# Turning the quantised feed-forward weights inside the attention stage, and moving the moments out of the feed-forward's turns

## The chip, the cores and the metric

The kernel runs on one core of a Trainium2 chip. The metric is the device time of one execution in microseconds (us); smaller is better.

## What is computed

Eight sequences of 384 tokens with 256 channels pass through two layers. Cut to what matters here:

```
h = concat(edge rows of the image, text)              # 8 x 384 x 256
h = h + attention0(layernorm(h))                      # 16 heads, two kinds of keys
h = h + feedforward0(layernorm(h))                    # blockwise FP4 of inputs, weights and hidden
h = h + attention1(layernorm(h))                      # 64 anchors for each of 16 heads
h = h + experts(layernorm(h))                         # one shared and one of eight experts

def fp4_quant_dequant(x):                             # blocks of 16 along the last axis
    scale = max(max|x| / 6, 1e-12)
    return nearest_grid(|x| / scale) * sign(x) * scale

def feedforward0(x):                                  # w_gate, w_up: 704 x 256; w_down: 256 x 704
    g, u = fp4(x) @ fp4(w_gate).T, fp4(x) @ fp4(w_up).T
    return fp4(silu(g) * u) @ fp4(w_down).T
```

## The kernel before

The program is written engine by engine, and each engine's list of instructions is run in its own order; semaphores join them. There are three stages (`attention0`, `middle`, `experts`), and between two of them `end_stage` clears the semaphores and holds all engines at a barrier. Tokens lie 128 to a tile: three tiles (`TT`) to an image, 24 tiles in all.

**attention0.** A turn works through 32 units (head and kind of key) of one image; TensorE, ScalarE (exponentials) and VectorE share it. The last turn has no next image to prepare, and from its unit 8 on VectorE rounds the three feed-forward weights there: `fp4_pads` and `fp4_step`, 36 steps in all (four passes of nine), which `fp4_part(v)` spreads evenly over 24 units. Behind the turn, `normalize` (VectorE), `turn_outputs`, `turn_y` and `output` (TensorE, all through PSUM bank 3), `copy_y` (ScalarE) and `add` (VectorE) finish the last image; `new_moments` and `gather_moments` take mean and variance. SyncE writes the rounded weights to a DRAM buffer, `fp4_dram`, half by half.

**middle, first block.** SyncE reads the rounded weights back, TensorE turns them in 36 transposes (`moves`), ScalarE copies them out of PSUM four at a time; ScalarE and VectorE make `rstd` of all 24 tiles.

**middle, second block: the feed-forward, then attention1.** For tile m (names as in the code):

- VectorE `inputs`: normalise (L1280), block maximum (L1265), scale (L1267), its inverse (L1269), divide (L1271).
- ScalarE `size_inputs` (L1694, L1696), then GpSimd `inputs` (L1440, L1442, L1444) round it by adding and subtracting; TensorE `turn_inputs` (L1503), ScalarE `copy_inputs` (L1677).
- TensorE `gate_up` in two halves (L1514, 8 matmuls each), ScalarE `silu` (L1689), VectorE `hidden` (two products at L1291, then the same L1265, L1267, L1269, L1271 on 704 columns).
- ScalarE `size_hidden` (L1700, L1702), GpSimd `hidden` (L1450, L1452, L1456), TensorE `turn_hidden` (L1523), ScalarE `copy_hidden` (L1683), TensorE `down` (L1530), VectorE `add` (L1305, and the `bn_stats` at L1307 with it).

The order on each engine is fixed by its `turn`: VectorE does `inputs` of tile m+2, `hidden` of m, `add` of m-2; ScalarE `size_hidden` m-1, `silu` m, `copy_hidden` m-2, `size_inputs` m+2, `silu` m, `copy_inputs` m+1; GpSimd `inputs` m+2, `hidden` m; TensorE `gate_up` m, `turn_hidden` m-2, `gate_up` m, `turn_inputs` m+1, `down` m-2. A hardware loop (`Fori`) runs six of the eight images. Behind it, the last tiles' work is mixed with the preparation of attention1: `anchor_part`, `scaled`, `scores`, `turn_weights`, `copy_weights`, and `roots` (Sqrt on ScalarE) with `inverses` (VectorE).

The buffers of the feed-forward lie in those of the experts' weights, `w12` and `w3`, which are made after attention0.

Of the kernel before, what the change touches and what calls it, by code (L numbers as in the profile page):

```python
# [13 lines left out]
P = 128  # L14
# [107 lines left out]
def attention0(nc, G, x, txt, scharr, wq, wk, wv, wkp, wo, alpha, wgate, wup, wdown, fp4_dram):  # L122
# [59 lines left out]
    with ExitStack() as ctx:  # L182
# [8 lines left out]
        xn = sb("xn", [P, TT, C])  # L191
        xT = sb("xT", [P, KC, T])
        parts = sb("parts", [P, 3, 3, KC, T], BF16)
        rest = sb("rest", [P, KC, T])
        qs = sb("qs", [P, 2, H0, T], BF16)
        ks = sb("ks", [P, 2, KINDS, H0, T], BF16)
# [45 lines left out]
        def side_of(i):  # L242
# [3 lines left out]
               yT[:].rearrange("p k t -> p (k t)")[:, 0:KC * C], rest[:].rearrange("p k t -> p (k t)")[:, 0:KC * C],  # L246
               xT[:].rearrange("p k t -> p (k t)")[:, 0:KC * C])]
# [9 lines left out]
        w4_in, w4_zero, w4_step, w4_out = sig("w_fp4_in"), sig("wzero"), sig("wstep", 9), sig("w_fp4_out")  # L257
# [38 lines left out]
        with nc.Block() as block:  # L296
            @block.sync
            def _(sp):
# [93 lines left out]
                for n in range(2):  # L392
                    sp.wait_ge(w4_step.sem, w4_step.at(2 * n + 2, 0))
                    s = slice(n * W0 // 2, (n + 1) * W0 // 2)
                    sp.dma_start(fp4_dram[:, s], w4[:, s]).then_inc(w4_out.sem, 16)
                sp.wait_ge(w4_out.sem, 32)
# [28 lines left out]
            def _(pool):  # L425
# [31 lines left out]
                add_kinds(B - 1, GROUPS // 2 - 1)  # L457

            @block.tensor
            def _(pe):  # L460
# [196 lines left out]
                for t in range(TT):  # L657
                    values(i, 1, GROUPS - 1, t)
                last = in_bank3("turn_outputs", i, GROUPS - 1, last)
                for k in range(KC):  # L660
                    last = in_bank3("turn_y", i, k, last)
                for n in range(2):
                    last = in_bank3("output", i, n, last)

            @block.scalar
            def _(act):
# [119 lines left out]
                for k in range(KC):  # L786
                    copy_y(B - 1, k)

            @block.vector
            def _(dve):  # L790
# [237 lines left out]
                normalize(B - 1, GROUPS - 1)  # L1028
                for n in range(2):
                    add(B - 1, n)  # L1030
# [13 lines left out]

def middle(nc, G, fp4_dram, wemb, wanc, wout, bout, E, w1s, w2s, w3s, W1, W2, W3):


    h, mv, rstd, ident, bn = G["h"], G["mv"], G["rstd"], G["ident"], G["bn"]
    with ExitStack() as ctx:
# [27 lines left out]
        wn = attn_flat[:, 0:W0]  # L1077
# [6 lines left out]
        room = {"w12": 0, "w3": 0}  # L1084

        def in_expert(of, *shape):

            flat = {"w12": E["w12"][:].rearrange("p b m k n -> p (b m k n)"), "w3": E["w3"][:].rearrange("p b a n -> p (b a n)")}[of]
            at, n = room[of], 1
            for s in shape:  # L1090
                n *= s
            room[of] = at + n
            names = "abc"[:len(shape)]
            if len(shape) == 1:
                return flat[:, at:at + n]
            return flat[:, at:at + n].rearrange("p (" + " ".join(names) + ") -> p " + " ".join(names),
                                                **dict(zip(names[1:], shape[1:])))

        wguT = in_expert("w3", 2 * KC, PAD0).rearrange("p (n k) c -> p n k c", n=2)
        wdT = in_expert("w3", IT0, C)  # L1100
        xb = in_expert("w3", TT, C)
        xm = in_expert("w3", TT, C)
        xT = in_expert("w12", TT, KC * P).rearrange("p t (k q) -> p t k q", k=KC)
        gate = in_expert("w12", 2, HALF0)
        hid = in_expert("w12", 2, INTER0)
        hq = in_expert("w12", TT, INTER0)
        hm = in_expert("w12", TT, INTER0)
        hz = in_expert("w12", TT, PAD0)
        hT = in_expert("w12", IT0, P)
        xs = in_expert("w12", TT, 3, C // BLOCK)  # L1110
        hs = in_expert("w12", TT, 3, INTER0 // BLOCK)
        tiny = in_expert("w12", INTER0 // BLOCK)
        floor = in_expert("w12", 1)

        w_in = [sig(f"w_f0_in{n}") for n in range(3)]
        turned, copied = sig("w0_t"), sig("w0_c")

        moves = []
        for n in range(2):
            for k in range(KC):  # L1120
                for a in range(IT0):
                    moves.append((n * NGU + a * C + k * P, wguT[:, n, k, a * P:(a + 1) * P]))
        for a in range(IT0):
            for o in range(KC):
                moves.append((2 * NGU + o * PAD0 + a * P, wdT[:, a, o * P:(o + 1) * P]))
        out_flat = [(wguT.rearrange("p n k c -> p (n k c)"), 2 * KC * IT0), (wdT.rearrange("p a c -> p (a c)"), IT0 * KC)]

        root_done, rstd_done = sig("root_f0"), sig("rstd_f0")

        with nc.Block() as block:  # L1130
            @block.sync
            def _(sp):
                for n in range(3):
# [10 lines left out]
            def _(pe):  # L1144
                for n, (at, _) in enumerate(moves):
                    bank = n // 4
                    if n % (len(moves) // 3) == 0:
                        pe.wait_ge(w_in[n // (len(moves) // 3)].sem, 16)
# [1117 lines left out]
```

## Time and profile before

| | us |
|---|---|
| median of 3 runs | 1908.77 |
| range of the runs | 1907.85 to 1909.83 |
| the profiled execution, its own time | 1910.5 |
| its span in the trace | 1908.7 |
| TensorE busy | 1774.1 (93%) |
| VectorE busy | 1025.9 (54%) |
| ScalarE busy | 679.3 (36%) |
| GpSimd busy | 398.9 (21%) |

The span is cut by the stages: attention0 until 739.95 us, the first block of middle until 753.42, the feed-forward from there until about 1000, then attention1 and the experts. A profile's percentages are averages over these stages. Names in its rows are those of the program with buffer numbers left out (`w` stands for `w12` and `w3`, `ps_a` and `ps_m` for PSUM in attention0 and middle); "PEld" is TensorE's weight load, and "SPq" is the queue of transfers that SyncE issues.

### The profile page before, as it was taken

How to read it: one execution, taken by the hardware profiler on the slowest of the kernel's cores; microseconds unless marked ns; L12 is line 12 of the kernel's file. 1: busy time of each engine (PE TensorE's matmuls, PEld its weight loads, DVE VectorE, ACT ScalarE, POOL GpSimd, SP SyncE). 2: the span in 40 equal slices, each digit the busy share in tenths (PEclk: the TensorE clock that was granted, in tenths of full speed). 3: DMA queues.
4: the chain of work that ended last, by engine and by line, in shares of the span. 5: the costliest groups of instructions: out<-in, count | busy, mean ns of one | idle time of the engine just before them, and what ended most of it. 6: DMA issues, size and time to landing. Idle time of an engine off the chain costs nothing. (4 is left out here: it accounts for less than half of the span.)

```text
span 1908.7 us, 29136 instructions
## 1 busy us (share of the span) xinstructions
PE 1774.1 (93%) x9935; PEld 1121.4 (59%) x9935; DVE 1025.9 (54%) x2071; ACT 679.3 (36%) x1292; POOL 398.9 (21%) x415
## 2 busy tenths in 40 slices
PE   7989999899999994888899999997999999999997
PEld 3324444444444333566665656565666668999997
DVE  6587877777778874788876445542321121222221
ACT  2115656556556673444444223322211110111110
POOL 2101021020210001677662211220032121010010
PEclk9979999999999996999999999998999999999999
DMA  5833643635436023000009000000010012242211
GB/s 186 137 51 64 88 76 39 103 62 65 76 61 91 2 71 126 19 0 0 0 6 375 3 0 0 0 1 1 0 42 33 17 36 97 101 167 99 100 36 32
DMA packets 112675, 117.56 MB, mean 62 GB/s; under 512 B 11535, under 2 KB 104513, under 8 KB 112322
## 3 DMA queue, kind: packets, MB, share of 16 engines
q1 hardware_dynamic: 99330, 87.93, 21.8%
q10 hardware_dynamic: 9600, 18.92, 2.8%
q0 software_dynamic: 3648, 9.46, 1.3%
q8 instruction: 55, 0.90, 0.2%
q14 instruction: 42, 0.34, 0.1%
HBM read 80.87 MB, written 35.29 MB: 61 GB/s over the span
## 5 line engine op out<-in xcount | busy, mean ns | idle before, releaser
L819 DVE TENSOR_REDUCE mx<-ps_a 128x1 f32<-128x384 f32 x768 | 383.6, 551 | 70.0 <-PE ps_a L503 67.8
L706 ACT ACTIVATE prob<-ps_a 128x768 f32<-128x768 f32 (+1 forms) x512 | 306.2, 650 | 119.8 <-PE ps_a L516 119.7
L503 PE MATMUL ps_a<-ks,qs 96*128 96x384 bf16 x768 | 221.6, 340 | 12.0 <-DVE mx L819 4.7
L516 PE MATMUL ps_a<-qs,ks 100*128 100x384 bf16 x768 | 210.3, 334 | 6.5 <-issue 3.8
L2029 PEld LDWEIGHTS ps_e<-xTr,w 128*128 128x128 f32 x1792 | 204.4, 192 | 2.2 <-issue 0.8
L2029 PE MATMUL ps_e<-xTr,w 128*128 128x128 f32 x1792 | 204.7, 275 | 0.6 <-DVE xTr L2202 0.6
L1965 PE MATMUL ps_e<-xT_all,w 128*128 (+1 forms) x512 | 170.4, 492 | 0.9 <-ACT xT_all L2056 0.9
L503 PEld LDWEIGHTS ps_a<-ks,qs 96*128 96x128 bf16 x768 | 61.9, 98 | 181.0 <-DVE mx L819 119.9
L527 PE MATMUL ps_a<-prob,vp 128*32 128x384 f32 x1536 | 164.7, 502 | 0.0
L1514 PE MATMUL ps_m<-w 128*128 128x352 f32 x384 | 125.0, 470 | 21.7 <-ACT w L1677 21.3
L1965 PEld LDWEIGHTS ps_e<-xT_all,w 128*128 128x128 f32 x512 | 97.7, 192 | 66.5 <-issue 1.8
L2092 ACT ACTIVATE gel_r<-ps_e 128x512 f32<-128x512 f32 x56 | 33.5, 597 | 280.5 <-PE ps_e L2029 280.5
L516 PEld LDWEIGHTS ps_a<-qs,ks 100*128 100x128 bf16 x768 | 72.0, 99 | 75.8 <-ACT prob L706 27.2
L2109 DVE TENSOR_TENSOR hid_e<-gel,ps_e 128x384 f32<-128x384 f32 x64 | 35.5, 554 | 137.1 <-ACT gel L2062 137.1
L1514 PEld LDWEIGHTS ps_m<-w 128*128 128x128 f32 x384 | 70.3, 192 | 61.8 <-issue 23.9
L2062 ACT ACTIVATE gel<-ps_e 128x384 f32<-128x384 f32 x64 | 31.5, 492 | 207.9 <-PE ps_e L1965 207.9
L2038 PE MATMUL ps_e<-w,hid_r 128*128 128x256 f32 x448 | 101.3, 379 | 0.0
L1476 POOL TENSOR_TENSOR attn<-lg,gsum 128x1024 f32<-128x1024 f32 x24 | 45.6, 1901 | 234.9 <-DVE gsum L1378 234.9
L2213 DVE TENSOR_TENSOR hid_r<-gel_r,ps_e 128x512 f32<-128x512 f32 x56 | 38.5, 688 | 100.6 <-ACT gel_r L2092 100.6
L1581 PE MATMUL ps_m<-wsT,xT_a 128*128 128x512 f32 x192 | 87.1, 596 | 4.8 <-DVE lg L1369 4.8
L442 POOL TENSOR_TENSOR y<-y 128x192 f32<-128x192 f32 x32 | 19.9, 621 | 332.5 <-DVE y L845 332.5
L2038 PEld LDWEIGHTS ps_e<-w,hid_r 128*128 128x128 f32 x448 | 82.9, 190 | 10.1
(242 smaller groups left out, 2519.7 us busy)
## 6 DMA issues: line engine op xcount, KB each, us to landing
ks<-parts_dram SPq DMA_DIRECT2D x192, 96.0 KB, 6.3
w<-in_L_ffn_W_dram ACTq DMA_DIRECT2D x18, 1024.0 KB, 8.2
parts_dram<-parts SPq DMA_DIRECT2D x24, 576.0 KB, 3.9
qs<-parts_dram SPq DMA_DIRECT2D x96, 96.0 KB, 4.2
prob<-in_x_dram SPq DMA_DIRECT2D x24, 256.0 KB, 3.6
w<-in_L_ffn_W_dram SPq DMA_DIRECT2D x6, 1024.0 KB, 13.0
grouped_x<-empty_row SPq DMA_DIRECT2D x1, 4352.0 KB, 24.6
grouped_h<-empty_row SPq DMA_DIRECT2D x1, 4240.5 KB, 33.1
```

What stands on the lines that cost most here:

```text
L503: mm = pe.matmul(ps[:, r % 3, 0:T], qs[0:NS, b, u // 2, t * P:(t + 1) * P], ks[0:NS, b, u % 2, u // 2], start=True, stop=True)
L516: mm = pe.matmul(ps[:, 4 + t, 0:T], ks[0:NS + 4, b, kp, hh, t * P:(t + 1) * P], qs[0:NS + 4, b, hh], start=True, stop=True)
L527: mm = pe.matmul(ps[j * SLOT:(j + 1) * SLOT, 7, 0:T], vp[:, b, t, g // 2 * QUAD + j], prob[:, g % 2, j, t], start=(t == 0), stop=(t == TT ...
L706: act.activation(prob[:, g % 2, j, ts.start:ts.stop], ps[:, 4 + ts.start:4 + ts.stop, 0:T], ACT.Exp).then_inc(exp_done.sem, 1)
L819: dve.tensor_reduce(at, ps[:, r % 3, 0:T], AX.X, ALU.max).then_inc(ring_free.sem, 1)
L1476: pool.tensor_tensor(attn[:, b, t].rearrange("p (h a) -> p h a", a=A1), lg[:, t % 2].rearrange("p (h a) -> p h a", a=A1), gsum[:, t % 2, 1 ...
L1514: mm = pe.matmul(ps[:, 2 * (u % 2) + n, 0:HALF0], xT[:, t, k], wguT[:, n, k, s * HALF0:(s + 1) * HALF0], start=(k == 0), stop=(k == KC - 1))
L1581: mm = pe.matmul(ps[:, bank + n], xT1[:, k, t * P:(t + 1) * P], wsT[:, k, n * 512:(n + 1) * 512], start=(k == 0), stop=(k == KC - 1))
L1965: mm = pe.matmul(ps[:, 2 * (a % 2) + m, 0:T], w12[:, 0, m, k, a * P:(a + 1) * P], xT_all[:, i, k], start=(k == 0), stop=(k == KC - 1))
L2029: mm = pe.matmul(ps[:, 2 * n + m, a * P:(a + 1) * P], w12[:, b, m, k, n * HALF1 + a * P:n * HALF1 + (a + 1) * P], xTr[:, k], start=(k == 0 ...
L2038: mm = pe.matmul(ps[:, 4, 0:C], hid_r[:, a], w3[:, b, a], start=(a == 0), stop=(a == IT1 - 1))
L2213: dve.tensor_tensor(hid_r[:, n * 4:(n + 1) * 4].rearrange("p a t -> p (a t)"), gel_r[:, n], ps[:, 2 * n + 1], ALU.mult).then_inc(rhid_done ...
```

## The change

1. The expert buffers are made before attention0. `parts`, `rest`, `xT`, `xn` and `ks` of attention0 now lie in `w3` and `w12` (sizes unchanged). The places of the feed-forward's tiles come from a new class, `FeedForwardTiles`, used in both stages.
2. `fp4_part` starts at unit 7 and ends at unit 29 (23 units in place of 24, from unit 8 to 31). The DRAM buffer, its two writes and three reads are gone, and with them the whole first block of middle.
3. In attention0's end TensorE turns the weights from where they were rounded, through banks 0, 1, 2, 4, 5, 6: 24 transposes ahead of the last `turn_outputs`, 12 behind it. ScalarE copies six banks ahead of `copy_y` 0 and three between `copy_y` 0 and 1. The roots of the first 21 tiles stand at the head of that, the last three's at the very end.
4. Also there: VectorE fills the pads, inverts 21 roots and does `inputs` of tile 0; ScalarE sizes it, GpSimd rounds it, TensorE turns it between `output` 0 and `output` 1, ScalarE copies it.
5. In the feed-forward `bn_stats` leaves `add`. Six tiles' moments are taken in the last turn; 18 `bn_stats` follow the turns, six each ahead of `scaled(0)`, `scaled(1)` and the first `less_max`. The second `roots` of ScalarE moves ahead of `copy_weights(0, 4)`. `anchors` moves behind the first tile's `hidden`.

```diff
+                for n in range(first, end):
+                    if n >= len(TURN_BANKS):
+                        pe.wait_ge(w4_copied.sem, n - len(TURN_BANKS) + 1)
+                    for q in range(4):
+                        mm = pe.transpose(ps[:, TURN_BANKS[n % len(TURN_BANKS)], q * P:(q + 1) * P], moves[4 * n + q], ident[:])
+                    mm.then_inc(w4_turned.sem, 1)
+                pe.wait_ge(exp_done.sem, exp_done.at(B, 0))
+                pe.wait_ge(w4_step.sem, w4_step.at(4, 0))
+                turn_feed_forward_weights(0, len(TURN_BANKS))
                 last = in_bank3("turn_outputs", i, GROUPS - 1, last)
+                turn_feed_forward_weights(len(TURN_BANKS), len(moves) // 4)
                 for k in range(KC):
                     last = in_bank3("turn_y", i, k, last)
-                for n in range(2):
-                    last = in_bank3("output", i, n, last)
+                last = in_bank3("output", i, 0, last)
+                pe.wait_ge(first_rounded.sem, 3)
+                pe.wait_ge(w4_copied.sem, len(moves) // 4)
+                for k in range(KC):
+                    mm = pe.transpose(ps[:, 4, k * P:(k + 1) * P], F.xb[:, 0, k * P:(k + 1) * P], ident[:])
+                mm.then_inc(first_turned.sem, 1)
+                last = in_bank3("output", i, 1, last)
...
-                for k in range(KC):
-                    copy_y(B - 1, k)
+                feed_forward_roots(0, B - 1)
+                copy_feed_forward_weights(0, len(TURN_BANKS))
+                copy_y(B - 1, 0)
+                copy_feed_forward_weights(len(TURN_BANKS), len(moves) // 4)
+                copy_y(B - 1, 1)
+                act.wait_ge(first_step.sem, 5)
...
+                feed_forward_roots(B - 1, B)
...
-                    n, units = 4 * w4_step.per, UNITS - 8
-                    return range(n * (v - 8) // units, n * (v - 7) // units) if v >= 8 else ()
+                    n, units = 4 * w4_step.per, UNITS - 9
+                    return range(n * (v - 7) // units, n * (v - 6) // units) if 7 <= v < 7 + units else ()
...
                     dve.tensor_tensor(h[:, n], h[:, n], ps[:, 5, 0:C], ALU.add).then_inc(h_done.sem, 1)
-                    dve.wait_ge(h_done.sem, h_done.at(i, t + 1))
-                    dve.bn_stats(bn[:, n], h[:, n]).then_inc(new_stats.sem, 1)
+                def stats(first, end):
+                    dve.wait_ge(h_done.sem, end)
+                    for n in range(first, end):
+                        dve.bn_stats(bn[:, n], h[:, n]).then_inc(new_stats.sem, 1)
...
-                        if last and t == 1:
-                            new_moments(0, EARLY_ROOTS)
+                        if first and t == 0:
+                            anchors()
+                        if last and t < 2:
+                            stats(t * TT, (t + 1) * TT)
+                            new_moments(t * TT, (t + 1) * TT)
...
                 inverses(0, 0, EARLY_ROOTS)
                 inputs1(0, 0)
+                stats(EARLY_ROOTS, EARLY_ROOTS + 6)
                 scaled(0)
                 add(B - 1, 1)
+                stats(EARLY_ROOTS + 6, EARLY_ROOTS + 12)
+                new_moments(EARLY_ROOTS, EARLY_ROOTS + 12)
                 scaled(1)
                 add(B - 1, 2)
-                new_moments(EARLY_ROOTS, NT)
+                stats(EARLY_ROOTS + 12, NT)
+                new_moments(EARLY_ROOTS + 12, NT)
...
                 copy_hidden(B - 1, 2)
+                roots(EARLY_ROOTS, NT)
                 copy_weights(0, 4)
...
-                roots(EARLY_ROOTS, NT)
                 for_pairs(act, turn1)
```

## Rows read from the trace of the kernel before

**Rows 1.** Windows: busy us (xinstructions) of PE, PEld, DVE, ACT, POOL; clock, DMA, GB/s

```profile
740.00:746.50 6.50, 0.00 (x0) 0.00 (x0) 0.30 (x1) 1.60 (x2) 0.00 (x0) 0.50 0.57 195
750.30:753.00 2.70, 2.29 (x20) 2.05 (x18) 0.00 (x0) 2.68 (x6) 0.00 (x0) 0.97 0.00 0
833.50:862.60 29.10, 25.93 (x108) 18.11 (x108) 24.50 (x40) 12.75 (x24) 20.86 (x19) 1.00 0.00 0
```

**Rows 2.** Timeline 784 to 969, TensorE: start, us, then what, idle time before it

```profile
784.02 2.53 PE L1514 MATMUL ps_m<-w 128*128 128x352 f32 x8
...
842.47 2.63 PE L1514 MATMUL ps_m<-w 128*128 128x352 f32 x8
...
848.19 2.76 PE L1530 MATMUL ps_m<-w 128*128 128x256 f32 x12
...
862.73 2.63 PE L1514 MATMUL ps_m<-w 128*128 128x352 f32 x8 [1.57 <-ACT w L1677]
...
968.90 2.63 PE L1514 MATMUL ps_m<-w 128*128 128x352 f32 x8 [1.24 <-ACT w L1677]
```

**Rows 3.** Timeline 855 to 875, VectorE and GpSimd

```profile
855.96 0.43 DVE L1307 BATCH_NORM_STATS2 bn<-h  x1 [0.15 <-DVE h L1305]
...
857.29 1.67 POOL L1450 TENSOR_TENSOR w<-w 128x704 f32<-128x704 f32 x1 [3.26 <-ACT w L1702]
857.32 1.68 DVE L1267 SCALAR_TENSOR_TENSOR w<-w 128x16 f32<-128x16 f32 x1
...
859.32 1.68 DVE L1271 SCALAR_TENSOR_TENSOR w<-w 128x256 f32<-128x256 f32 x1
...
865.01 0.89 DVE L1271 SCALAR_TENSOR_TENSOR w<-w 128x704 f32<-128x704 f32 x1
...
868.19 1.48 DVE L1271 SCALAR_TENSOR_TENSOR w<-w 128x256 f32<-128x256 f32 x1
...
873.32 0.89 DVE L1271 SCALAR_TENSOR_TENSOR w<-w 128x704 f32<-128x704 f32 x1
```

**Rows 4.** Timeline 697 to 761: the end of attention0 to the first gate_up

```profile
697.28 1.99 PE L550 MATMUL ps_a<-wT,yT 128*128 128x256 f32 x8
...
724.23 1.36 DVE L904 TENSOR_TENSOR ks<-ks,qs 128x1152 f32<-128x1152 f32 x1
...
731.43 3.75 PE L550 MATMUL ps_a<-wT,yT 128*128 128x256 f32 x8 [0.66 <-ACT yT L696]
...
735.96 2.07 PE L550 MATMUL ps_a<-wT,yT 128*128 128x256 f32 x4 [0.78 <-DVE h L854]
...
739.64 0.31 DVE L867 BATCH_NORM_AGGREGATE mv<-bn 128x2 f32<-128x6 f32 x3
741.80 2.44 SPq L1135 DMA_DIRECT2D attn<-fp_weights  x3
...
754.30 0.49 DVE L1280 SCALAR_TENSOR_TENSOR w<-h,mv,rstd 128x256 f32<-128x256 f32 x1
...
759.00 0.62 POOL L1444 TENSOR_TENSOR w<-w 128x256 f32<-128x256 f32 x1
...
760.84 6.60 PE L1514 MATMUL ps_m<-w 128*128 128x352 f32 x16 [0.46 <-ACT w L1677]
```

**Rows 5.** Timeline 758 to 773: the anchors' copies, and tile 0's first rounding

```profile
758.64 0.98 DVE L1328 COPY gs<-ps_m 64x64 f32<-64x64 f32 x4
...
772.86 1.67 POOL L1450 TENSOR_TENSOR w<-w 128x704 f32<-128x704 f32 x1 [4.14 <-ACT w L1702]
```

**Rows 6.** Timeline 995 to 1018: behind the last turn

```profile
995.22 1.22 DVE L1333 TENSOR_SCALAR wsT<-ps_m 128x1024 f32<-128x1024 f32 x1 [0.90 <-PE ps_m L1548]
...
996.78 2.83 PE L1530 MATMUL ps_m<-w 128*128 128x256 f32 x12 [0.94 <-DVE wsT L1333]
...
1003.08 1.23 DVE L1365 TENSOR_REDUCE gmax<-ps_m 128x16 f32<-128x1024 f32 x1 [2.00 <-PE ps_m L1581]
...
1017.03 1.28 ACT L1726 ACT_TABLE_LOAD   x1
```

More of the change, by code:

```diff
@@ L119, with __init__, of, flat_buffer @@
 KINDS = 2
-def attention0(nc, G, x, txt, scharr, wq, wk, wv, wkp, wo, alpha, wgate, wup, wdown, fp4_dram):
+class FeedForwardTiles:
+    def __init__(self, E):
+        self.E, self.room = E, {"w12": 0, "w3": 0}
+        self.wguT = self.of("w3", 2 * KC, PAD0).rearrange("p (n k) c -> p n k c", n=2)
+        self.wdT = self.of("w3", IT0, C)
+        self.xb = self.of("w3", TT, C)
+        self.xm = self.of("w3", TT, C)
+        self.xT = self.of("w12", TT, KC * P).rearrange("p t (k q) -> p t k q", k=KC)
+        self.gate = self.of("w12", 2, HALF0)
+        self.hid = self.of("w12", 2, INTER0)
+        self.hq = self.of("w12", TT, INTER0)
+        self.hm = self.of("w12", TT, INTER0)
+        self.hz = self.of("w12", TT, PAD0)
+        self.hT = self.of("w12", IT0, P)
+        self.xs = self.of("w12", TT, 3, C // BLOCK)
+        self.hs = self.of("w12", TT, 3, INTER0 // BLOCK)
+        self.tiny = self.of("w12", INTER0 // BLOCK)
+        self.floor = self.of("w12", 1)
+    def of(self, buffer, *shape):
+        flat = flat_buffer(self.E, buffer)
+        at, n = self.room[buffer], 1
+        for s in shape:
+            n *= s
+        self.room[buffer] = at + n
+        names = "abc"[:len(shape)]
+        if len(shape) == 1:
+            return flat[:, at:at + n]
+        return flat[:, at:at + n].rearrange("p (" + " ".join(names) + ") -> p " + " ".join(names),
+                                            **dict(zip(names[1:], shape[1:])))
+def flat_buffer(E, name):
+    return E["w12"][:].rearrange("p b m k n -> p (b m k n)") if name == "w12" else E["w3"][:].rearrange("p b a n -> p (b a n)")
+def attention0(nc, G, E, x, txt, scharr, wq, wk, wv, wkp, wo, alpha, wgate, wup, wdown):
     h, mv, rstd, bn, ident, eps = G["h"], G["mv"], G["rstd"], G["bn"], G["ident"], G["eps"]
@@ L785, in _, with feed_forward_roots, copy_feed_forward_weights @@
                 copy_outputs(B - 1, GROUPS - 1)
-                for k in range(KC):
-                    copy_y(B - 1, k)
+                def feed_forward_roots(first, end):
+                    act.wait_ge(hm_done.sem, hm_done.at(end, 0))
+                    tiles = slice(first * TT, end * TT)
+                    act.activation(rstd[:, tiles], mv[:, tiles, 1], ACT.Sqrt, bias=eps[:]).then_inc(root1_done.sem, 1)
+                def copy_feed_forward_weights(first, end):
+                    for n in range(first, end):
+                        act.wait_ge(w4_turned.sem, n + 1)
+                        act.copy(turned_to[n], ps[:, TURN_BANKS[n % len(TURN_BANKS)]]).then_inc(w4_copied.sem, 1)
+                feed_forward_roots(0, B - 1)
[4 more added lines that the diff above has]
+                act.wait_ge(first_step.sem, 5)
+                act.activation(F.xm[:, 0], F.xb[:, 0], ACT.Square, scale=BEND).then_inc(first_sized.sem, 1)
+                act.wait_ge(first_sized.sem, 1)
+                act.activation(F.xm[:, 0], F.xm[:, 0], ACT.Identity, bias=F.floor).then_inc(first_sized.sem, 1)
+                act.wait_ge(first_turned.sem, 1)
+                act.copy(F.xT[:, 0].rearrange("p k t -> p (k t)"), ps[:, 4, 0:C]).then_inc(first_copied.sem, 1)
+                feed_forward_roots(B - 1, B)
             @block.vector
@@ L1110, in middle @@
[L1110 to L1122, printed above, removed]
@@ L1305, in add @@
                     dve.tensor_tensor(h[:, n], h[:, n], ps[:, 5, 0:C], ALU.add).then_inc(h_done.sem, 1)
-                    dve.wait_ge(h_done.sem, h_done.at(i, t + 1))
-                    dve.bn_stats(bn[:, n], h[:, n]).then_inc(new_stats.sem, 1)
+                def stats(first, end):
+                    dve.wait_ge(h_done.sem, end)
+                    for n in range(first, end):
+                        dve.bn_stats(bn[:, n], h[:, n]).then_inc(new_stats.sem, 1)
                 def new_moments(first, end):
@@ L1536, in turn @@
                         gate_up(i, t, 0)
+                        if first and t == 0:
+                            pe.wait_ge(an_in.sem, 32)
+                            pe.transpose(ps[:, 7, 0:A1], an2.rearrange("p n d -> p (n d)"), ident[0:A1, 0:A1]
+                                         ).then_inc(an_t.sem, 1)
                         if before:
```

170 lines of the change are left out of this document (75 added, 95 removed).

## The prediction, made before the changed kernel was run

> **What bounds the kernel now.** I read three views: the windows (busy time by stage), then the timeline of the two places that the change touches, then the ends of waits in it. The boundary between attention0 and the feed-forward is an empty stretch for TensorE: in 6.5 us it has nothing, and only the weights' transfer runs [rows 1]. The first feed-forward matmul starts at 760.84, 20.9 us behind attention0's last aggregation at 739.95 [rows 4].
>
> In the feed-forward TensorE is busy 25.93 of 29.1 us an image at full clock [rows 1], so neither the clock nor its work is the whole bound. A tile without a wait takes 8.51 us (842.47 to the end of `down` at 850.95), but from 784.02 to 968.90 there are 19 tiles in 184.88 us, 9.73 each; the waits, 1.57 and 1.24 in the rows shown, are for ScalarE's copy of the next inputs [rows 2]. ScalarE is not busy: it waits for VectorE's `inputs` two tiles ahead. VectorE in turn is held by GpSimd. The `inputs` scale on 16 columns (L1267) takes 1.68 us, because it begins 0.03 us behind GpSimd's 1.67 us L1450, and ends with it; the next L1271 then falls under GpSimd's following instruction, another 1.68 us [rows 3]. I call that a slow tile. In the tile after it L1267 slips in ahead of L1450, and only L1271 is held, 1.48 us [rows 3]. From the end of one hidden L1271 (865.90) to the next (874.21) this fast tile takes 8.31 us; the slow one, from 855.48, took 10.42. An image has two slow and one fast: 29.15, which is its length.
>
> The Trainium skill ("GPSIMD Engine Reference", Specifications) says that GpSimd shares its SBUF interfaces with VectorE and contends with instructions of two SBUF inputs; the trace agrees, 1.68 us for a 16-column operation.
>
> **Part by part.** *Moments out of the turns.* `bn_stats` with its wait for `add` sits between `add` and `inputs`: L1280 starts 0.96 us behind the add; without it some 0.4. So 0.5 us go from VectorE's chain. What matters is the alignment: GpSimd's L1450 starts 1.81 us behind the end of the hidden L1271 (857.29 against 855.48), through ScalarE's two sizes, and `inputs`' L1267 at 1.84 [rows 3]. 0.5 us earlier it is at 1.3, clear of L1450 in every tile. L1271 of `inputs` then comes at about 1.8 and is held at worst as in the fast tile. VectorE's loop is then 8.31 us and whatever GpSimd's remaining instructions add; TensorE's is 8.51 and becomes the bound. GpSimd and VectorE share about 6.8 + 2.2 us of two-input work a tile, partly overlapped in the holds, so I do not take the floor but 8.65, nearer to it than to the 9.73 because no long hold but one is left. 19 tiles: 184.9 - 164.4 = 20.5 us. Bounds: 23.2 us (8.51) and nothing.
>
> At a loop's turn L1280 has had an extra 0.4 us for branch and registers behind `bn_stats`. I expect it hidden, since VectorE no longer waits for `add` just ahead of the branch; if it isn't, that is the second case below.
>
> *The boundary.* Today: rounding ends at 725.59, `output` 0 starts at 731.43 (5.84 later), the stage ends at 739.95, SyncE is released at 741.80 (1.85 of barrier) [rows 4].
> New rounding end: one step is done a unit earlier, in an idle stretch (about 1.4 gained), but two more steps now stand ahead of the `add` and `normalize` that TensorE waits for, which gives most of it back. I take 725.0; bounds 724.2 and 726.
> - 24 transposes at 0.115 (20 in 2.29 [rows 1]) are 2.8; a `normalize` of 0.65 runs beside them: +2.15 ahead of the last `turn_outputs`.
> - Three weight copies between `copy_y` 0 and 1, beside the second `turn_y`: +0.6. Full clock for the small transposes gives 0.3 back.
> - `output` 0 starts at 725.0 + 5.84 + 2.15 + 0.6 - 0.3 = 733.3. It takes 3.75 today, 1.99 in mid-stage [rows 4]. TensorE's clock is 1.2 GHz there today, after 4 us in which it waited for the rounding; now the transposes fill that stretch. I take 1.99: 735.3.
> - Tile 0: VectorE's 1.9 us lies beside the copies; what follows it took 3.4 (754.30 + 1.9 to 759.62 [rows 4]) and starts behind `copy_y` 1, at 733.2: 736.6, two transposes 0.4, `output` 1 at 737.0. Its 2.07 becomes 1.1 at full clock: 738.1. `output` 1 is thus held 1 us by the rounding of tile 0, not by the `add` of `output` 0.
> - add, stats, aggregation as today 1.92 (738.03 to 739.95), the last roots 0.3: 740.3. Barrier 1.85, first instruction 0.2: `gate_up` at 742.35.
> Gain 760.84 - 742.35 = 18.5; at low clock both outputs cost 1.6 more, 16.9. The rest of the first block (transfer, turning, copies, second block's start) is simply not there, and the SyncE queue has only attention1's loads left, which nobody in the first tile waits for but the anchors.
>
> *The ramp.* Tile 1's `inputs` now start with `gate_up` 0 instead of ahead of it; TensorE needs them 5.4 us on and has 6.6 us of work [rows 4], so hidden. `anchors` is not: today its 1.3 us (copies 0.98 [rows 5]) lie ahead of the turns; behind tile 0's `hidden` they push `inputs` of tile 3 past the start of GpSimd's L1450 (772.86 today, 1.8 behind L1271 [rows 5]). That makes one slow tile (10.42 - 8.31 = 2.1) and the 1.3 beside it, less a little: -3.2. Bounds 0 and -4.5.
>
> *The tail.* `add` 22, six `bn_stats` (0.43 alone [rows 3], an estimated 0.36 from start to start when they follow each other, 2.2) and 12 aggregations (0.85) come ahead of `scaled(1)`, for which TensorE already waits 0.94 [rows 6]: 3.05 against a gap of 1.3, so 1.7 late, of which the earlier `inverses` (no `bn_stats` ahead of it) gives 0.3 back. The six ahead of `scaled(0)` lie in VectorE's idle time there. The last six and their aggregation (2.7) end about when the scores do, against 2.00 us of idle time plus the 1.4 already lost [rows 6]: nothing. In the last turn VectorE has no `inputs`, so the early moments are covered. -1.4, and 0.4 won in the last turn: -1.0. Bounds +0.4 and -3. The moved roots remove a table load of 1.28 us at 1017.03 [rows 6] and the one behind it; ScalarE is idle there: nothing.
> The Trainium skill ("ScalarE: Activation LUTs", What ACT_TABLE_LOAD costs) puts a switch of sets at 2.66 us, with a drain beyond the load. No drain stands ahead of the load at 1017.03, which begins as the exponential before it ends. By either figure this sum stays as it is, if the earlier Sqrt's set is still loaded; if the moved roots loaded their set anew, the page's figure would add about 2.7 in front of the weights' copies, and the row's 1.3.
>
> Attention0's turns and everything behind 1018 are unchanged work; the buffers' new addresses I take at nothing, bounds 0 and -2.
>
> **Sum.** 18.5 - 3.2 + 20.5 - 1.0 = 34.8 us. The span of 1908.7 belongs to an execution of 1910.5, the median is 1908.77; I take the difference off the median: **1874.0 us**.
>
> **Rivals.**
> *One slow tile per image stays* (the loop's turn, or a GpSimd instruction that now runs into L1267). Speaks for it: margins of 0.1 to 0.5 us decide. Per tile (8.51 + 8.51 + 10.42) / 3 = 9.15, 19 x 0.58 = 11.1 in place of 20.5: 1883.4. Chance 0.20.
> *The pattern stays at 9.73*, because VectorE and GpSimd together are the bound and the holds only move: `bn_stats` has one input and was never held, so its removal may just lengthen a hold. Gain 14.3: 1894.5. Against it: the fast tile exists and has nothing but the 0.5 us in its favour. Chance 0.11.
> *Slower:* L1267 and L1271 of `inputs` are held in every tile, and the hidden L1271 too by the rest of one more GpSimd instruction, an estimated 0.8: 10.42 + 0.8 = 11.2 a tile, 19 x 1.47 = 27.9 lost against 14.3 won, 1922. It decides from a mean of 9.73 + 14.3 / 19 = 10.5 us a tile. For it: a GpSimd that never idles meets every VectorE operation; against it: GpSimd has 28% idle time [rows 1]. Chance 0.05, and 0.02 for a mean so near 10.5 that nothing shows.
> My forecast has 0.60, a floor of 8.51 with nothing lost in the ramp 0.02 (1868).
>
> **Range and chances.** Likeliest case alone: 1868 to 1881. To 1892 it takes in the second case and part of the third, with the low clock and the longer ramp: 1868 to 1892. Faster by over 0.2% (3.8 us, about what a measurement of this kernel can tell from no change): 0.60 + 0.02 + 0.20 + 0.11 = 0.93; same 0.02; slower 0.05.
>
> **What would show it.** Right: `gate_up` starts some 18 us earlier; from tile 3 on TensorE has no wait over 0.3 us and tiles are 8.5 to 8.8 us; L1267 on 16 columns is below 0.6 us everywhere; TensorE's `output` 0 takes 2 us. Wrong: a tile period with a 10.4 in it; `inputs`' L1267 still at 1.7; a `down` of the last tile waiting far over 2.4 us for `scaled(1)`; an attention0 that ends after 742. What would upset it most is the order in which L1271 and L1450 meet, which no row of before shows in this order.

## The result and the profile after

| | before | after |
|---|---|---|
| median, us | 1908.31 (4 runs) | 1863.76 (4 runs) |
| range of the runs, us | 1900.93 to 1909.83 | 1862.18 to 1865.91 |
| the profiled execution, its span | 1908.7 | 1860.4 |
| ratio, 95% interval | | 0.978 [0.9759, 0.98] |

The kernel is 44.5 us faster by the medians and 48.3 by the spans; 34.8 were forecast. Two more sets of runs of the changed kernel gave 0.9803 [0.9774, 0.9833] and 0.9806 [0.9793, 0.982], that is 36 and 38 us by the medians. What differs between them is told below. In the experiments two runs far above the others of their kernel, 4581.26 us in e3 and 1908.95 us in e11, are left out of the ratios. Line numbers moved: `gate_up` is now L1574, `turn_hidden` L1583, `turn_inputs` L1563, `down` L1590, VectorE's `inputs` L1330, L1315, L1317, L1319, L1321 (the last four also in `hidden`), its products L1341, GpSimd's `inputs` L1499 to L1503 and `hidden` L1509, L1511, L1515, ScalarE's `copy_inputs` L1738, `scaled` L1387.

**The loop.** Windows of the changed kernel: busy us of PE, PEld, DVE, ACT, POOL, then the clock; the last row is the loop, and answers to the third of [rows 1].

```profile
744.00:750.00 6.00, 3.59 (x14) 2.14 (x12) 5.67 (x12) 2.02 (x3) 2.95 (x2) 1.00 0.37 141
750.00:756.00 6.00, 3.68 (x7) 2.19 (x8) 4.98 (x9) 1.96 (x5) 3.85 (x5) 0.61 0.00 0
780.00:811.00 31.00, 31.00 (x138) 22.80 (x137) 26.41 (x45) 16.50 (x31) 27.72 (x23) 1.00 0.00 0
```

TensorE has no idle time in these 31 us, and GpSimd, which had 28% idle time, has 11%. The timeline of VectorE and GpSimd in one tile answers to [rows 3]:

```profile
796.91 0.89 DVE L1321 SCALAR_TENSOR_TENSOR w<-w 128x704 f32<-128x704 f32 x1
797.72 0.41 DVE L1355 TENSOR_TENSOR h<-h,ps_m 128x256 f32 x1
798.05 0.62 DVE L1330 SCALAR_TENSOR_TENSOR w<-h,mv,rstd 128x256 f32 x1
...
799.16 0.17 DVE L1317 SCALAR_TENSOR_TENSOR w<-w 128x16 f32<-128x16 f32 x1
...
799.62 1.67 POOL L1509 TENSOR_TENSOR w<-w 128x704 f32<-128x704 f32 x1 [0.47 <-ACT w L1763]
799.66 1.92 DVE L1321 SCALAR_TENSOR_TENSOR w<-w 128x256 f32<-128x256 f32 x1
...
802.95 0.52 DVE L1341 TENSOR_TENSOR w<-w,ps_m 128x352 f32<-128x352 f32 x1 [0.94 <-ACT w L1750]
```

L1317 on 16 columns takes 0.17 us, because it starts 0.46 us ahead of GpSimd's L1509; only L1321 is held, 1.92 us to L1509's end and a little beyond. VectorE then even waits 0.94 us for `silu`: it is no longer the bound. From the inputs of tile 4 on L1317 on 16 columns takes 0.17 or 0.18 us in every tile, and from those of tile 6 on L1321 takes 1.91 to 1.93.

**The ramp.** TensorE's timeline, with the first and the last tile of the loop:

```profile
752.32 5.06 PE L1574 MATMUL ps_m<-w 128*128 128x352 f32 x8 [4.73 <-ACT w L1738]
...
763.50 2.53 PE L1574 MATMUL ps_m<-w 128*128 128x352 f32 x8
...
919.94 2.53 PE L1574 MATMUL ps_m<-w 128*128 128x352 f32 x8
```

From 763.50 to 919.94 there are 19 tiles, 8.23 us each: the `down`s follow each other at 8.20, but for two steps of 8.42 and 8.59. Ahead of them tile 2 waits 4.73 us, and its eight matmuls take 5.06 in place of 2.53. The granted clock was 1.00 in the wait until 750.0, 0.79 from there to 752.3 and 0.50, the 1.2 GHz level, under these matmuls. VectorE, GpSimd and ScalarE during that wait:

```profile
745.16 0.27 DVE L1377 MEMSET gs<- 128x256 f32 x1
745.46 0.98 DVE L1382 COPY gs<-ps_m 64x64 f32<-64x64 f32 x4
746.48 0.48 DVE L1330 SCALAR_TENSOR_TENSOR w<-h,mv,rstd 128x256 f32<-128x256 f32 x1
...
746.97 1.67 POOL L1509 TENSOR_TENSOR w<-w 128x704 f32<-128x704 f32 x1 [4.30 <-ACT w L1763]
747.45 1.22 DVE L1317 SCALAR_TENSOR_TENSOR w<-w 128x16 f32<-128x16 f32 x1
...
748.99 1.67 DVE L1321 SCALAR_TENSOR_TENSOR w<-w 128x256 f32<-128x256 f32 x1
...
750.70 0.42 ACT L1755 ACTIVATE w<-w 128x256 f32<-128x256 f32 x1 [3.45 <-DVE w L1321]
...
751.90 0.36 ACT L1738 COPY w<-ps_m 128x256 f32<-128x256 f32 x1
```

The anchors (1.28 us) push L1330, the inputs of tile 3, to 746.48. L1317 then falls into L1509 and L1321 into L1511: a slow tile. TensorE waits for other inputs, those of tile 2. It had turned them by 747.59, but in ScalarE's order their copy (L1738) stands behind `size_inputs` of tile 3 (L1755), which waits 3.45 us for that late L1321.

**The boundary and the tail.** TensorE from the end of the rounding to the first `gate_up`, which answers to [rows 4], and then around `scaled(1)` [rows 6]:

```profile
718.29 2.81 PE L730 MATMUL ps_a<-ident,w 128*128 128x128 f32 x24 [3.01 <-DVE w L1010]
...
726.00 1.97 PE L614 MATMUL ps_a<-wT,yT 128*128 128x256 f32 x8 [1.40 <-ACT yT L779]
...
729.33 1.03 PE L614 MATMUL ps_a<-wT,yT 128*128 128x256 f32 x4
734.71 4.08 PE L1574 MATMUL ps_m<-w 128*128 128x352 f32 x8 [4.35 <-ACTq L1780]
...
947.95 4.19 PE L1590 MATMUL ps_m<-w 128*128 128x256 f32 x12 [2.09 <-DVE wsT L1387]
```

The rounding ends at 718.14 and `gate_up` starts 16.57 us later (17.35 forecast, 35.25 before). `output` 0 takes 1.97 us at full clock. In the tail `down` of the last tile waits 2.09 us for `scaled(1)`, and takes 4.19 in place of 2.83. Here the granted clock was still 1.00 in the wait and fell only behind it, to a mean of 0.66 from 947.95 to 952.10. That this does not follow from the length of the wait alone is shown under e6.

### The profile page after: what moved, and what is told of

Same layout as the page of the kernel before. It is cut to its first block and busy times, and to the rows that moved or that the text cites. A ratio compares the mean times of both kernels' runs of the same rounds, so it can differ in the third digit from the quotient of the medians.

```text
span 1860.4 us, 29106 instructions
## 1 busy us (share of the span) xinstructions
PE 1757.0 (94%) x9935; PEld 1118.6 (60%) x9935; DVE 1007.1 (54%) x2072; ACT 674.2 (36%) x1289; POOL 407.2 (22%) x415
## 5 line engine op out<-in xcount | busy, mean ns | idle before, releaser
L567 PE MATMUL ps_a<-w,qs 96*128 96x384 bf16 x768 | 220.1, 338 | 12.3 <-DVE mx L925 5.2
L580 PE MATMUL ps_a<-qs,w 100*128 100x384 bf16 x768 | 208.8, 332 | 6.1 <-issue 3.4
L567 PEld LDWEIGHTS ps_a<-w,qs 96*128 96x128 bf16 x768 | 61.4, 98 | 180.8 <-DVE mx L925 116.6
L1574 PE MATMUL ps_m<-w 128*128 128x352 f32 x384 | 125.8, 472 | 9.8 <-ACT w L1738 5.3
L580 PEld LDWEIGHTS ps_a<-qs,w 100*128 100x128 bf16 x768 | 71.9, 99 | 74.0 <-ACT prob L789 26.3
L1574 PEld LDWEIGHTS ps_m<-w 128*128 128x128 f32 x384 | 72.6, 195 | 44.7 <-ACT w L1738 6.3
L496 POOL TENSOR_TENSOR y<-y 128x192 f32<-128x192 f32 x32 | 19.9, 621 | 332.5 <-DVE y L951 332.5
L2099 PEld LDWEIGHTS ps_e<-w,hid_r 128*128 128x128 f32 x448 | 82.9, 190 | 10.1
```

What stands on the lines that cost most here:

```text
L567: mm = pe.matmul(ps[:, r % 3, 0:T], qs[0:NS, b, u // 2, t * P:(t + 1) * P], ks[0:NS, b, u % 2, u // 2], start=True, stop=True)
L580: mm = pe.matmul(ps[:, 4 + t, 0:T], ks[0:NS + 4, b, kp, hh, t * P:(t + 1) * P], qs[0:NS + 4, b, hh], start=True, stop=True)
L1574: mm = pe.matmul(ps[:, 2 * (u % 2) + n, 0:HALF0], xT[:, t, k], wguT[:, n, k, s * HALF0:(s + 1) * HALF0], start=(k == 0), stop=(k == KC - 1))
L2099: mm = pe.matmul(ps[:, 4, 0:C], hid_r[:, a], w3[:, b, a], start=(a == 0), stop=(a == IT1 - 1))
```

## The experiments

Each kernel's profiled execution is cut at three points: the last product of the means in attention0 (`mneg`, ahead of the rounding's last steps), the first `gate_up` and the first of attention1's scores. All in us:

| | last mneg | to gate_up | to scores | to the end | span |
|---|---|---|---|---|---|
| before | 666.63 | 94.21 | 238.60 | 909.26 | 1908.7 |
| before again (e4) | 666.34 | 91.59 | 238.38 | 908.79 | 1905.1 |
| addresses alone (e3) | 663.45 | 94.22 | 238.70 | 909.23 | 1905.6 |
| moments alone (e1) | 662.38 | 91.37 | 210.67 | 908.08 | 1872.5 |
| all but the moments (e2) | 660.81 | 76.12 | 242.50 | 907.47 | 1886.9 |
| after | 660.37 | 74.34 | 217.22 | 908.47 | 1860.4 |
| after again (e5) | 666.58 | 78.01 | 218.38 | 908.43 | 1871.4 |
| after, third (e9) | 665.19 | 77.49 | 217.14 | 908.48 | 1868.3 |
| anchors in the gap (e6) | 666.52 | 74.18 | 211.10 | 908.80 | 1860.6 |
| scaled first (e7) | 666.07 | 76.04 | 214.97 | 907.92 | 1865.0 |
| statistics in the gap (e8) | 661.13 | 77.55 | 215.20 | 908.72 | 1862.6 |
| both gaps (e10) | 660.81 | 76.87 | 210.48 | 907.84 | 1856.0 |
| anchors gap, scaled first (e11) | 665.03 | 76.11 | 210.80 | 908.06 | 1860.0 |
| statistics behind add (e12) | 661.18 | 76.03 | 216.63 | 908.66 | 1862.5 |

### e1: the moments alone

The kernel before with `bn_stats` out of `add`, and the tail's statistics and `roots` in the order of the changed kernel; the boundary and the place of `anchors` as before.

```diff
-                    dve.wait_ge(h_done.sem, h_done.at(i, t + 1))
-                    dve.bn_stats(bn[:, n], h[:, n]).then_inc(new_stats.sem, 1)
...
+                stats(EARLY_ROOTS, EARLY_ROOTS + 6)
                 scaled(0)
                 add(B - 1, 1)
+                stats(EARLY_ROOTS + 6, EARLY_ROOTS + 12)
+                new_moments(EARLY_ROOTS, EARLY_ROOTS + 12)
                 scaled(1)
```

> The kernel before with the moments' part alone: bn_stats out of the feed-forward's add, 18 of them behind the turns, the second roots moved. Alignment theory: the scale on 16 columns is never held, a tile takes 8.20 us as in the changed kernel, the whole gains about 27 us (28.4 in 19 tiles, less 1.5 in the tail): ratio 0.986. Work theory (VectorE's busy time is the bound and bn_stats is 0.43 us of it): 0.45 us a tile, 10 us in all, ratio 0.995, and slow tiles of 10.4 us still there.

Measured: 1874.5 us, 0.985 [0.9832, 0.9867], beside a before of 1904.25. The stretch from `gate_up` to the scores falls from 238.6 to 210.67, so some 28 us come from this part alone, as the alignment theory had it (about 27 in all; 29.75 by the medians). Windows of this kernel, in the same stretch as the third of [rows 1]:

```profile
833.50:862.60 29.10, 29.10 (x129) 21.41 (x128) 25.10 (x44) 13.92 (x27) 26.21 (x23) 1.00 0.00 0
```

TensorE's busy time goes from 25.93 to 29.10 of 29.1 us.

### e2: everything but the moments

The changed kernel with `bn_stats` back in `add`, and the tail as before.

> The changed kernel with bn_stats back behind the add in every turn, and the tail as before. Alignment theory: the pattern of two slow tiles and one fast is back, 29.1 us an image, about 27 us slower than the changed kernel and 18 to 20 faster than the one before: ratio to before 0.990. Work theory: 10 us slower than the changed kernel, ratio 0.982.

Measured: 1890.68 us, 0.9934 [0.9917, 0.9951]. The gain of the boundary is there (76.12 us from mneg to `gate_up`), and the old pattern is back: 18 tiles from 770.95 to 944.89, 9.66 us each, with steps between `down`s of 10.4, 10.1 and 8.6. The ratio is above the expected 0.990. Part of that is the slow ramp of the changed kernel, which this one keeps: 28.41 us from the first `gate_up` to that of tile 3, where the kernel before has 23.18. VectorE and GpSimd of this kernel:

```profile
777.67 0.43 DVE L1357 BATCH_NORM_STATS2 bn<-h  x1 [0.16 <-DVE h L1355]
778.07 0.49 DVE L1330 SCALAR_TENSOR_TENSOR w<-h,mv,rstd 128x256 f32 x1
...
779.00 1.67 POOL L1500 TENSOR_TENSOR w<-w 128x704 f32<-128x704 f32 x1 [3.26 <-ACT w L1754]
779.04 1.66 DVE L1317 SCALAR_TENSOR_TENSOR w<-w 128x16 f32<-128x16 f32 x1
```

L1317 starts 0.04 us behind GpSimd and takes 1.66: the slow tile of [rows 3] within 0.02 us. From `gate_up` to the scores e1 gains 27.9 us and e2 loses 3.9, 24.0 together, where the changed kernel gains 21.4. So the two halves disturb each other a little, by 2.6 us.

### e3 and e4: where attention0's 6.3 us come from

In the first profile after, the last mneg comes 6.26 us earlier than before. e3 is the kernel before with only the buffers moved into `w3` and `w12`; e4 is the kernel before, word for word.

> The kernel before with only the buffers of attention0 laid into w3 and w12, nothing moved. Address theory: the first turns are 6 us shorter as in the changed kernel (last mneg at 660.4 in place of 666.6), ratio 0.997. Start-up theory (the 6 us are a difference between executions, from the first transfers): no difference to before beyond the spread of its runs, ratio 0.999 to 1.001.

> The kernel before, word for word, for a second trace of it. Start-up theory: its first turns land anywhere between the two traces, last mneg between 660 and 667. Address theory: the last mneg within 1 us of 666.6 again.

Measured: e3 1903.99 us, 0.9996 [0.9985, 1.0008]; e4 one run, 1906.84. The addresses change nothing that these runs show. The last mneg is at 662.4 to 666.6 us in the four profiles with the old boundary and at 660.4 to 666.6 in the ten with the new one (means 664.7 and 663.4), and for the changed kernel alone at 660.37, 666.58 and 665.19. It is a spread between executions. It arises early: the first mneg comes at 105.3 to 111.5 us, and from the first to the second pass 28.5 to 31.6 us. Here are windows of two executions of the changed kernel (the first, and e5):

```profile
110.00:120.00 10.00, 8.48 (x28) 3.16 (x28) 9.54 (x24) 0.00 (x0) 0.00 (x0) 1.00 0.06 7
```

```profile
110.00:120.00 10.00, 8.44 (x21) 2.90 (x20) 8.36 (x21) 0.00 (x0) 0.00 (x0) 0.79 0.41 49
```

Where the clock is 0.78 or 0.79 in these 10 us, 31.6 us pass from the first mneg to the second (before, e4, e5, e6, e7); where it is 0.83, 30.0 (e2, e8, e10, e12); where it is 1.00, 28.5 (after, e1, e3, e9, e11). That they go together was seen; what makes the clock fall at one time or the other was not settled. The third profile of the changed kernel, e9, has the short step and is late because its first mneg is (111.5 against 106.8).

### e5 and e9: the changed kernel again

> The changed kernel word for word, as the base for the three kernels beside it: 1863.8 us and a ratio of 0.978, first gate_up at 734 to 737 us, and from there to the first scores 217 us. If the variation of the first turns is one of the start-up (theory), the last product of the means in attention0 comes at another time than 660.4 (660 to 667 were seen), and everything behind it moves by the same amount; if the new addresses caused the earlier time of the changed kernel (rival), it is 660.4 again within 0.3.

> The changed kernel word for word, the base for the kernels beside it: 1862 to 1870 us, ratio 0.978 to 0.980.

Measured: 1869.37 (0.9803) and 1865.97 us (0.9806). The last mneg at 666.58 speaks for the spread. In e5 there is a second one: the boundary takes 78.01 us, not 74.34. TensorE of e5:

```profile
726.50 4.48 PE L730 MATMUL ps_a<-ident,w 128*128 128x128 f32 x24 [2.77 <-DVE w L1010]
```

The 24 transposes took 2.81 us in the first profile and 4.48 here, as the clock was at half for most of them (0.62 on average from 726.5 to 731.0); the rounding itself ended 2 us later against mneg. So the length of the boundary varies between executions, before (91.4 to 94.2) as after (74.2 to 78.0). The means over 4 and 10 profiles are 92.85 and 76.27: a gain of 16.6 us, where my first pair of profiles shows 19.9.

### e6: anchors where VectorE waits

In the changed kernel VectorE waits 2.25 us between tile 0's two products. The anchors go there.

```diff
                         dve.tensor_tensor(hid[:, t % 2, s * HALF0:(s + 1) * HALF0], gate[:, u % 2], ps[:, 2 * (u % 2) + 1, 0:HALF0],
                                           ALU.mult).then_inc(hid_done.sem, 1)
+                        if isinstance(i, int) and i == 0 and t == 0 and s == 0:
+                            anchors()
...
-                        if first and t == 0:
-                            anchors()
```

> The changed kernel with anchors moved from behind tile 0's hidden to between the two products of tile 0's hidden, where VectorE waited 2.25 us (739.84 to 742.09). Theory (the anchors push the chain of tiles 1 to 3 into GpSimd's instructions, and the clock of TensorE falls in the wait that this makes): the wait of 4.7 us at tile 2 goes to under 2, the clock stays up there, and from gate_up of tile 0 to that of tile 3 it is 23 to 25 us in place of 28.8: 4 to 5.6 us faster than the changed kernel, ratio to the kernel before 0.975 to 0.976. Rival (the wait at tile 2 comes from tile 1's inputs that now start only with gate_up 0, so the anchors' place does not matter): 28 us or more for these three tiles, and no change of the time beyond 1 us.

Measured: 1861.92 us, 0.9774 [0.9756, 0.9793], beside 0.9803 for the changed kernel on the same chip. The intervals overlap, but the traces don't leave it open: from `gate_up` to the scores 211.10 us, where three profiles of the changed kernel have 217.1 to 218.4. TensorE of e6, at tile 2 and tile 3:

```profile
754.76 2.63 PE L1574 MATMUL ps_m<-w 128*128 128x352 f32 x8 [1.17 <-ACT w L1738]
...
764.15 2.53 PE L1574 MATMUL ps_m<-w 128*128 128x352 f32 x8
```

The wait is 1.17 us in place of 4.73, the clock stays up, and tile 3 starts 23.45 us behind the first `gate_up` (740.70) in place of 28.79. The anchors' place cost 5.3 us.

Another 1.3 us of e6's gain lies in the tail, where nothing was changed. The last `down` waits as long as in the changed kernel, but runs at full clock:

```profile
949.10 2.86 PE L1590 MATMUL ps_m<-w 128*128 128x256 f32 x12 [2.09 <-DVE wsT L1389]
```

e1 shows the same (2.86 us behind a wait of 2.09), while the three profiles of the changed kernel show 4.19, 4.54 and 4.14 behind it. What decides between the two was not settled.

### e7: scaled(1) first in the tail

```diff
                 add(B - 1, 1)
+                scaled(1)
                 stats(EARLY_ROOTS + 6, EARLY_ROOTS + 12)
                 new_moments(EARLY_ROOTS, EARLY_ROOTS + 12)
-                scaled(1)
                 add(B - 1, 2)
```

> The changed kernel with scaled(1) ahead of the six statistics and twelve aggregations that stand before it in the tail. Theory (they make TensorE wait 2.1 us for the inputs' transposes, and the fall of the clock costs another 1.4 in the last down): from gate_up of tile 22 to the first scores 29.5 us or less in place of 32.0, so 2 to 3 us faster than the changed kernel, if the statistics find room in the idle time before the logits. Rival (VectorE is then late with its last statistics and inverses, and the wait moves to the scores' maxima): the first scores come 1 to 3 us earlier but the end of the kernel stays within 1 us of the changed kernel's.

Measured: 1865.36 us, 0.9788 [0.9768, 0.9808]; by the time alone it can't be told from the changed kernel. In the trace `down` of the last tile waits 0.94 us again, and takes 2.83:

```profile
954.42 2.83 PE L1590 MATMUL ps_m<-w 128*128 128x256 f32 x12 [0.94 <-DVE wsT L1387]
```

`gate_up` to scores falls to 214.97, and nothing is given back behind the scores (907.92). The expected 2 us are there in the trace: some 1.15 us of wait, and 1.36 us that the slow `down` no longer loses.

### e8 and e12: is it the work or its place?

Both put one `bn_stats` a tile back into the turns. e8 puts it between the two products of `hidden`, where VectorE waits anyway; e12 puts it between `add` and `inputs` again, as before, but for the previous tile, so that it waits for nothing. Both keep only the statistics of the last three tiles for the end of the last turn and the tail. The insertion in e8 (in e12 the same three lines follow `add`):

```diff
+                        if s == 0 and not (isinstance(i, int) and i == 0):
+                            m = (i - 1) * TT + t
+                            dve.wait_ge(h_done.sem, h_done.at(i - 1, t + 1))
+                            dve.bn_stats(bn[:, m], h[:, m]).then_inc(new_stats.sem, 1)
```

> The changed kernel with each tile's bn_stats back in the turns, but between the two products of hidden, where VectorE waits for ScalarE's second silu for about 0.94 us, and not between the add and the next inputs; the tail keeps only three statistics. By alignment (theory: only the place of the delay against GpSimd's instructions matters) a tile stays at 8.2 to 8.3 us, the tail is up to 3 us shorter, and the kernel is 1 to 3 us faster than the changed kernel. By work (rival: VectorE's 24 statistics must leave the turns) a tile takes 8.2 + 0.45 or the old pattern of 9.1 to 9.7, and the kernel is 8 to 25 us slower than the changed kernel.

> The changed kernel with one bn_stats a turn back between add and inputs, but that of the tile before, so that it waits for nothing and delays inputs by about 0.35 us in place of 0.63. In the changed kernel the 16-column L1317 starts 0.46 us ahead of GpSimd's L1509. Alignment by the start (theory): it then starts about 0.1 us ahead of L1509 and is not held, a tile stays at 8.20 to 8.3 us and the kernel within 2 us of the changed one. Rival A (it must have ended, or must have 0.3 us of room): L1317 is held to the end of L1509 in two tiles of three and a tile takes 9.5 to 9.8 us as before, ratio 0.992 to 0.995. Rival B (work counts, not place): 0.35 us a tile, 8.55 us, 7 us slower than the changed kernel.

Measured: e8 1864.11 us, 0.9793 [0.9767, 0.9818], beside 1869.37 and 0.9803 for the changed kernel in the same set; e12 1868.72, 0.9816 [0.9803, 0.9828], beside 1865.97 and 0.9806. By the times alone neither can be told from the changed kernel. In both traces the `down`s again follow each other at 8.20 us in most steps, and 19 tiles take 8.24 and 8.26 us each (8.23 in the changed kernel). VectorE and GpSimd of e12:

```profile
800.53 0.42 DVE L1400 BATCH_NORM_STATS2 bn<-h  x1
800.87 0.47 DVE L1330 SCALAR_TENSOR_TENSOR w<-h,mv,rstd 128x256 f32 x1
...
801.83 0.17 DVE L1317 SCALAR_TENSOR_TENSOR w<-w 128x16 f32<-128x16 f32 x1
...
802.10 1.67 POOL L1513 TENSOR_TENSOR w<-w 128x704 f32<-128x704 f32 x1 [0.28 <-ACT w L1767]
```

L1317 starts 0.27 us ahead of GpSimd and is not held; in e2 it starts 0.04 behind and takes 1.66. The same instruction in the same place costs next to nothing in e12, and 1.4 us a tile in e2 (9.66 against 8.26): what differs is its wait for `add`, a few tenths of delay.

All fourteen traces bear this out. From the first `gate_up` to the scores VectorE runs the 16-column scale 318 times. The 216 that started while GpSimd had no `tensor_tensor` under way took 0.17 or 0.18 us, even with GpSimd's next one 0.03 us away. The 102 that started inside one ended 0.03 to 0.08 us behind it, however long that took.

Against e8, e12 loses 1.4 us between `gate_up` and scores. It is one more meeting with GpSimd, in the tail: VectorE normalises three tiles for attention1 (L1418). In e8 all three operations start ahead of GpSimd's L1513 and take 1.06 us; in e12 the third starts inside it and the three take 2.43. TensorE waits 2.51 us for them in place of 0.93.

```profile
941.79 2.43 DVE L1418 TENSOR_SCALAR xn_a<-h,mv,rstd 128x256 f32<-128x256 f32 x3
```

### e10 and e11: the gains together

e10 is e6 and e8 together, e11 is e6 and e7.

> The changed kernel with each tile's bn_stats between the two products of hidden (one image later), the tail with three statistics left, and anchors between the two products of tile 0. If both gains stand beside each other (theory: the ramp gains 5.5, the tail 2.0), from the first gate_up to the first scores it is 209.5 us in place of 217.2, and the kernel is 6 to 8 us faster than the changed kernel: ratio 0.975 to 0.976. Rival (bn_stats in the ramp takes the room that anchors leave, so a GpSimd instruction holds VectorE there again): 213 us or more, and no better than anchors in the gap alone (211.1).

> The changed kernel with anchors between the two products of tile 0 and scaled(1) ahead of the six statistics. Both gains add (theory): 217.2 - 6.1 - 2.0 = 209.1 us from the first gate_up to the first scores, 6 to 8 us faster than the changed kernel. Rival: the two gains share a cause (the clock) and the second gives nothing, 211 us.

Measured: e10 1858.54 us, 0.9768 [0.9755, 0.9781], and e11 1859.86, 0.9764 [0.9752, 0.9777], beside the changed kernel's 1865.97, 0.9806 [0.9793, 0.982]. Both beat both kernels, by 6 to 7 us (0.4% by the ratios) against the changed one. From `gate_up` to the scores they have 210.48 and 210.80, where 209.5 and 209.1 were expected and e6 alone has 211.10. In the profiles the second gain adds only 0.3 to 0.6 of its 2 us. The tail of e11 is as short as that of e7: from the `down` three ahead of the last to the scores 23.92 us (928.02 to 951.94) and 23.92 (933.16 to 957.08). But e6 takes only 25.13 there, where the changed kernel takes 26.38: its last `down` ran at full clock, so 1.25 of the 2 us were in its 211.10 already. e11 is 1.2 us shorter there than e6, and gives 0.8 back in the ramp (24.25 us to tile 3 against 23.45), where the eight matmuls behind the barrier took 4.91 us in e11 and 4.09 in e6. The sum expected for e11 counted the clock's part of the tail twice; e10 lacks 0.7 of its gain in the ramp and the loop, not in the tail.

## Why the forecast fell short

**The loop: the mechanism was right, the term too small.** Forecast 20.5 us at 8.65 us a tile, measured 28.4 at 8.23 (184.88 - 156.44). This is the step that failed: TensorE's floor of 8.51 us, and the 0.14 us put on it. The alignment came out as written: L1317 clear of GpSimd in every tile of the loop, L1321 held once. e1, e2, e8 and e12 show that this is the cause. Two things were mis-sized. The floor of 8.51 was taken from a tile of before that I called one without a wait; where TensorE really never waits, its period is 8.20 us, because the steps from `gate_up` to `turn_hidden` (2.37) and from `down` to `gate_up` (2.59) were each 0.1 to 0.2 longer in that tile. That is 0.31 of the difference, 5.9 us over 19 tiles. (The rows named for the 8.51, 842.47 to 850.95, give 8.48; it is 8.51 from the end of the `down` before, at 842.44.) The other 0.14 was my allowance for work that VectorE and GpSimd share: the hold of 1.92 us leaves VectorE 0.94 us idle, so nothing of it reaches TensorE. In e1, e6, e10 and e11 this division takes 0.57 to 0.59 us for six or seven tiles early in the loop and some 1.92 later, and the `down`s come at 8.20 in both. Two longer steps (8.42 and 8.59) give 0.03 a tile back. With the 28.4 in the place of 20.5 the sum gives 1866.1, beside the 1863.8 to 1869.4 of the three sets.

**The ramp: right sign, too small.** Forecast -3.2 (bound -4.5), measured -5.6 (28.79 against 23.18 in the profile of before). The slow tile from the anchors is there as described, and e6 removes it. What was left out is the clock: behind the wait of 4.73 us it is at half level, and eight matmuls cost 2.5 us more.

**The boundary: right, its clock only at times.** Forecast 18.5, or 16.9 at low clock; 19.9 in the first pair of profiles, 16.6 as a mean over all. In the first profile `output` 0 took 1.97 us (1.99 forecast) and the 24 transposes 2.81 (2.8 forecast), but that is not the rule. Over the ten profiles with the new boundary `output` 0 took 1.96 or 1.97 in six and 3.05 to 3.26 in four (e2, e7, e11, e12), and the transposes took 2.81 in two (the first, and e6) and 4.12 to 5.36 in eight. The transposes do not always keep the clock up, as the forecast had it; its low-clock case of 16.9 is the one that the mean supports.

**The tail: right in number, in part by luck.** Forecast -1.0, measured -1.45 (31.99 us from `gate_up` of tile 22 to the scores, against 30.54). The statistics delay `scaled(1)` by 1.15 us (a wait of 2.09 for 0.94), where 1.4 were forecast. The slower `down` adds 1.36, which the forecast left out. What hides it is some 1.1 us that came back ahead of the last `down`, where 0.4 were forecast: up to the `down` three ahead of the last the stretch is 0.46 shorter, and a later step between two `down`s is 7.03 in place of 7.59. No run isolates the removed table load; behind the scores the changed order is 0.3 to 0.8 us shorter.

**Attention0's turns: "nothing" was right, and the first comparison misled.** Its 6.26 us are a spread between executions (e3, e4, e5). Sum of what belongs to the change: 16.6 - 5.6 + 28.4 - 1.45 + 0.8 = 38.7 us, which is what the two later sets of runs show (36 and 38). In the first set the kernel before ran 3 to 4 us longer than in those (1908.31 against 1905.14 and 1904.08), and the changed one 2 to 6 us shorter; both are within the spread seen between profiles of one kernel. Against these 38.7 us the forecast of 34.8 is 3.9 us short: 7.9 in the loop and 0.8 behind the scores, less 1.9 in the boundary, 2.4 in the ramp and 0.45 in the tail. The measured median lies 4 us under the range's fast end, 1868, which was the floor of 8.51 with nothing lost in the ramp. With the sum of the parts the kernel comes to 1870.1, and the remaining 6 us down to the 1863.76 of the first set lie within the spread between sets, which no term of the forecast allowed for.

Of the rivals, "one slow tile per image stays" and "the pattern stays" fall with the 8.23 us a tile, and the slower case with them. That VectorE's and GpSimd's work was the bound, the reason given for the pattern's staying, is refuted by e8 and e12: 21 of 24 statistics done in the turns, and 19 tiles within 0.5 us of the changed kernel's.

## What to carry to other kernels

Where two engines hold each other up, look at which instruction starts first, not at the sum of their work: an instruction of 0.4 us with a wait cost 1.4 us a tile in one place, and next to nothing when it waited for nothing or lay in a gap. Take a floor for TensorE from the lengths of its own steps where it is really busy throughout, not from the best tile of a stretch with waits in it. And price a wait of TensorE of two us or more with the slower matmuls behind it: here they cost 1.3 us behind a wait of 2.09 and 2.5 us behind one of 4.73, and in some executions nothing behind the shorter one. Profile such a stretch more than once.

## What the runs showed of the hardware

- Behind a wait of 4.73 us ahead of `gate_up` the next eight matmuls took 5.06 us for 2.53 in the changed kernel, and 4.24 to 5.06 in the seven profiles with that wait. Behind one of 2.09 us twelve of `down` took 4.14 to 4.54 us in three profiles (after, e5, e9) and 2.86 in two (e1, e6), with a granted clock of 1.00 over the wait in all five. After 1.17 us (e6) and 0.94 us (e7) they ran at full clock.
- VectorE's 16-column L1317 took 0.17 us when it started 0.27 us ahead of GpSimd's instruction, and 1.66 when 0.04 behind. L1321 on 256 columns, which started 0.04 us behind GpSimd's 1.67 us, took 1.92: the hold can outlast that instruction. `bn_stats`, with one input, took 0.40 to 0.43 wherever it stood. In these rows the order of the starts decides over a factor of ten. The Trainium skill ("GPSIMD Engine Reference", Specifications) says that GpSimd shares its SBUF interfaces with VectorE; the trace agrees, 1.66 us for a 16-column operation.
- The same kernel has executions 6 us apart in their first third, and 4 us in the boundary; a part of this goes with a different granted clock over a few us (0.79 for 1.00 from 110 to 120 us, and under the 24 transposes). A single pair of profiles can't tell a gain of that size.
